# A causal attention block: the mask of the transposed scores comes with the shift that starts the score bank, instead of from a product on TensorE

## The reference, cut to what matters

```
x: (1, 2048, 256), H = 16 heads, D_NOPE + D_ROPE = 192, D_V = 128
h      = layernorm(x) * (1 + ca) + sa
q, k   = low-rank projections of h, with rotary parts     # 16 heads, 192 wide
scores = einsum('bhsd,bhtd->bhst', q, k) * scale
scores = where(tril(ones(seq, seq)), scores, finfo.min)    # causal: key t <= query s
attn   = softmax(scores, axis=-1)
out    = einsum('bhst,bhtd->bhsd', attn, v);  x = x + ga * (out @ w_o)
# then a second norm and a mixture of 8 experts, 2 per token
```

## Time and profile before

| | us |
|---|---|
| median of 3 runs (1333.61 to 1336.11) | 1335.11 |
| the profiled execution, its own time | 1335.97 |
| its span | 1334.2 |
| PE busy in the span | 1212.8 (91%) |
| DVE busy | 887.8 (67%) |
| ACT busy | 790.3 (59%) |
| POOL busy | 689.4 (52%) |

### The profile page before, as it was taken

One profiled execution on the slowest core, in us unless ns is written; L12 is line 12 of the kernel. 1 busy time (PEld: TensorE's weight loads), 2 busy tenths in 40 slices (PEclk: granted clock), 3 DMA queues, 4 the chain that ended last, 5 costly groups with the idle time before them and its releaser, 6 DMA issues. The chain is left out here.

```text
span 1334.2 us, 24515 instructions
## 1 busy us (share of the span) xinstructions
PE 1212.8 (91%) x9452; PEld 959.9 (72%) x9452; DVE 887.8 (67%) x1836; ACT 790.3 (59%) x1166; POOL 689.4 (52%) x569
## 2 busy tenths in 40 slices
PE   2766999999999999999999999999999958989897
PEld 2654577777777677777777777777777757878786
DVE  2533667777676777767667776766767476677776
ACT  1152577677777777777776777777777633322232
POOL 0121376677666657676665767666686741111100
PEclk9876799999999999999999999999999978999998
DMA  9201002001000200100020010002000040000000
GB/s 275 75 0 57 16 1 57 2 17 41 17 17 1 57 1 17 42 17 17 2 57 1 17 42 17 17 2 57 1 17 1 2 158 1 1 16 0 16 16 16
DMA packets 57671, 39.54 MB, mean 30 GB/s; under 512 B 7744, under 2 KB 57152, under 8 KB 57408
## 3 DMA queue, kind: packets, MB, share of 16 engines
q1 hardware_dynamic: 51216, 33.94, 8.7%
q10 hardware_dynamic: 6352, 4.19, 1.3%
HBM read 33.66 MB, written 4.46 MB: 29 GB/s over the span
## 5 line engine op out<-in xcount | busy, mean ns | idle before, releaser
L768 DVE TENSOR_REDUCE gates<-bank 128x1 f32<-128x512 f32 (+3 forms) x640 | 384.8, 609 | 225.7 <-PE bank L841 149.4
L660 POOL TENSOR_TENSOR pt_lo<-pt 128x1024 f16<-128x1024 f32 x192 | 372.7, 1946 | 241.8 <-ACT pt L717 240.5
L717 ACT ACTIVATE pt<-pair 128x1024 f32<-128x1024 f32 x192 | 196.1, 1021 | 130.1 <-PE pair L866 129.1
L708 ACT ACTIVATE pair<-shift 128x1024 f32<-128x1024 f32 x256 | 263.4, 1029 | 11.9
L884 PE MATMUL bank<-values,pt 128*128 128x129 f16 x2176 | 235.2, 222 | 9.4 <-DVE rowsum L800 9.3
L884 PEld LDWEIGHTS bank<-values,pt 128*128 128x128 bf16 x2176 | 191.5, 97 | 61.7 <-issue 31.8
L886 PE MATMUL bank<-values,pt_lo 128*128 128x65 f16 x2176 | 223.9, 193 | 0.0
L666 POOL TENSOR_TENSOR pt_lo<-pt 128x512 f16<-128x512 f32 (+3 forms) x256 | 178.8, 720 | 58.9 <-ACT pt L721 58.4
L886 PEld LDWEIGHTS bank<-values,pt_lo 128*128 128x128 f16 x2176 | 193.8, 98 | 0.0
L721 ACT ACTIVATE pt<-pair 128x512 f32<-128x512 f32 (+3 forms) x256 | 111.3, 436 | 77.4 <-PE pair L869 77.1
L841 PE MATMUL bank<-kt_a_hi,q_hi 128*128 128x512 f32 (+2 forms) x320 | 132.4, 419 | 4.4 <-ACT q_hi L690 2.4
(11 more groups left out here) (217 smaller groups left out, 2341.1 us busy)
## 6 DMA issues: line engine op xcount, KB each, us to landing
turn_by<-rope_cos_by_feature SPq DMA_DIRECT2D x64, 128.0 KB, 3.0
turn_by<-rope_sin_by_feature SPq DMA_DIRECT2D x64, 128.0 KB, 3.0
xs<-in_L_attn_x ACTq DMA_DIRECT2D x1, 2048.0 KB, 25.2
lat<-in_L_attn_w_o SPq DMA_DIRECT2D x1, 2048.0 KB, 26.6
xs_again<-in_L_attn_x SPq DMA_DIRECT2D x1, 2048.0 KB, 8.1
out<-xs_again SPq DMA_DIRECT2D x4, 512.0 KB, 2.8
lat<-in_L_wmod SPq DMA_DIRECT2D x1, 1536.0 KB, 16.1
lat<-in_L_attn_w_qb SPq DMA_DIRECT2D x1, 1152.0 KB, 8.0
```

Source lines behind the costliest of these rows:

```text
L660: pool.tensor_tensor(out=pt_lo[:, at].rearrange("p a n -> p (a n)"), in0=full, in1=cut(full), op=ALU.subtract).then_inc(low_ok, 1)
L708: act.activation(s_pair[u % 2][:, :, :], shift[:, item % SHIFTS:item % SHIFTS + 1, :].to_broadcast([P, 2, BW]), ACT.Copy).then_inc(seeded[ ...
L717: act.activation(pt[:, at], s_pair[u % 2][:, :, :], ACT.Exp).then_inc(exp_done, 1)
L768: dve.tensor_reduce(out=mx[:, item % MAXIMA, t, part:part + 1], in_=work_of(w)[:, 0:n * P], axis=AXX, op=ALU.max).then_inc(work_seen["v"], 1)
```

## The change

The 256 mask products (L869) go. In their place the shift that starts a score bank already holds the mask in the triangle. POOL makes a transposed triangle `mask_t` once at the start of `attend`. After ACT has copied the shift of an item, DVE reads the same work bank again and writes `diag_shift` = shift + log(1024) + mask for all four query tiles (`diagonal_rows`, one 128x512 instruction per item). A work bank with a shift in it is therefore free for PE only when ACT and DVE have both read it. The seed of a `d = 0` unit on ACT is now three instructions (the shift for columns 256 and up of both halves, the shift for tile 1 of half 0, and the two triangle tiles from `diag_shift`); that of a `d = 2` unit on DVE is two (the two triangle tiles, and the shift for tile 3 of half 0). The `shift` tile has 3 slots instead of 4.

```diff
-PT_RING, SHIFTS, Q_SLOTS, MAXIMA = 4, 4, 3, 4
+PT_RING, SHIFTS, Q_SLOTS, MAXIMA = 4, 3, 3, 4
@@ seen_by
-    return {"max": "v", "shift": "a", "q": "va"}[use[0]] if use[0] != "q" or use[2] < 2 else ""
+    return {"max": "v", "shift": "av", "q": "va"}[use[0]] if use[0] != "q" or use[2] < 2 else ""
@@ attend
+        def diagonal_of(u):
+            d = UNITS[u][2]
+            return s_pair[u % 2][:, :, :].rearrange("p a (b n) -> p (a b) n", n=P)[:, d:d + BT + 2:BT + 1, :]
@@ POOL
+                pool.memset(mask_t[:, :], 0.0).then_inc(consts_ok, 1)
+                pool.wait_ge(consts_ok, 2)
+                pool.affine_select(out=mask_t[:, :], in_=mask_t[:, :], compare_op=ALU.is_ge, fill=MASKED, base=0,
+                                   pattern=[[1, P]], channel_multiplier=-1).then_inc(consts_ok, 1)
@@ ACT seed
-                    act.activation(s_pair[u % 2][:, :, :], shift[:, item % SHIFTS:item % SHIFTS + 1, :].to_broadcast([P, 2, BW]),
-                                   ACT.Copy).then_inc(seeded["a"], 1)
+                    if UNITS[u][2] is None:
...
+                    else:
+                        act.activation(s_pair[u % 2][:, :, 2 * P:], shift[:, at:at + 1, 2 * P:].to_broadcast([P, 2, 2 * P]),
+                                       ACT.Copy).then_inc(seeded["a"], 1)
+                        act.activation(s_pair[u % 2][:, 0, P:2 * P], shift[:, at, P:2 * P], ACT.Copy).then_inc(seeded["a"], 1)
+                        act.activation(diagonal_of(u), diag_shift[:, item % 2, 0:2, :], ACT.Copy).then_inc(seeded["a"], 1)
@@ DVE
+                def diagonal_rows(item):
+                    n = WORK[("shift", item)]
+                    dve.wait_ge(work_seen["a"], SEEN["a"][n + 1])
+                    if item >= 2:
+                        dve.wait_ge(seeded["a"], SEEDS["a"][FIRST_UNIT[item - 1]])
+                    dve.scalar_tensor_tensor(out=diag_shift[:, item % 2], in0=work_of(n).rearrange("p (t n) -> p t n", n=P),
+                                             scalar=math.log(P_SCALE), in1=mask_t[:, :].unsqueeze(1).to_broadcast([P, BT, P]),
+                                             op0=ALU.add, op1=ALU.add).then_inc(work_seen["v"], 1)
@@ DVE seed
-                    dve.tensor_copy(s_pair[u % 2][:, :, 2 * P:],
-                                    shift[:, item % SHIFTS:item % SHIFTS + 1, 2 * P:].to_broadcast([P, 2, 2 * P])).then_inc(seeded["v"], 1)
+                    dve.tensor_copy(diagonal_of(u), diag_shift[:, item % 2, 2:BT, :]).then_inc(seeded["v"], 1)
+                    dve.tensor_copy(s_pair[u % 2][:, 0, 3 * P:], shift[:, at, 3 * P:]).then_inc(seeded["v"], 1)
@@ DVE rounds, behind the maxima and the spread, ahead of query work and seed
+                    if r in SHIFT_AT:
+                        diagonal_rows(SHIFT_AT[r])
@@ PE scores
-                        last = pe.matmul(to, keys[a], q[b], start=False, stop=(m == 2 and d is None), skip_group_check=True)
-                    if d is not None:
-                        on = (d + half) * P
-                        last = pe.matmul(s_pair[u % 2][:, half, on:on + P], mask16[:, :], ident16[:, :], start=False, stop=True,
-                                         skip_group_check=True)
+                        last = pe.matmul(to, keys[a], q[b], start=False, stop=(m == 2), skip_group_check=True)
```

More of the change, by code:

```diff
@@ L115 @@
 OPS = [0, *itertools.accumulate(1 if d is None else 2 for _, _, d in UNITS)]
-SEEDS = {e: [0, *itertools.accumulate(seed_on_vector(u) == (e == "v") for u in range(NU))] for e in "av"}
+SEEDS = {"a": [0, *itertools.accumulate({None: 1, 0: 3, 2: 0}[d] for _, _, d in UNITS)],
+         "v": [0, *itertools.accumulate(2 * (d == 2) for _, _, d in UNITS)]}
 ENDS = [0, *itertools.accumulate(d is not None for _, _, d in UNITS)]
@@ L585, in attend @@
         nmx = sb(own, "nmx", [P, 2, BT])
+        diag_shift = sb(own, "diag_shift", [P, 2, BT, P])
+        mask_t = sb(own, "mask_t", [P, P], BF16)
         spread = sb(own, "spread", [P, 2, BT, P], F32R)
@@ L695, in shift_rows @@
                     if item >= SHIFTS:
-                        act.wait_ge(seeded["v"], item - SHIFTS + 1)
+                        act.wait_ge(seeded["v"], 2 * (item - SHIFTS + 1))
                     act.activation(shift[:, item % SHIFTS, :], work_of(n)[:, :], ACT.Copy,
@@ L707, in seed @@
                         act.wait_ge(opened, 1)
-                    act.activation(s_pair[u % 2][:, :, :], shift[:, item % SHIFTS:item % SHIFTS + 1, :].to_broadcast([P, 2, BW]),
-                                   ACT.Copy).then_inc(seeded["a"], 1)
+                    at = item % SHIFTS
+                    if UNITS[u][2] is None:
+                        act.activation(s_pair[u % 2][:, :, :], shift[:, at:at + 1, :].to_broadcast([P, 2, BW]),
+                                       ACT.Copy).then_inc(seeded["a"], 1)
+                    else:
+                        act.activation(s_pair[u % 2][:, :, 2 * P:], shift[:, at:at + 1, 2 * P:].to_broadcast([P, 2, 2 * P]),
+                                       ACT.Copy).then_inc(seeded["a"], 1)
+                        act.activation(s_pair[u % 2][:, 0, P:2 * P], shift[:, at, P:2 * P], ACT.Copy).then_inc(seeded["a"], 1)
+                        act.activation(diagonal_of(u), diag_shift[:, item % 2, 0:2, :], ACT.Copy).then_inc(seeded["a"], 1)
                 def exponentials(u):
```

2 lines of the change are left out of this document (1 added, 1 removed).

## The result

Over 13 runs each the changed kernel has a median of 1337.84 us (1335.68 to 1339.36), the kernel before 1335.08 us (1333.01 to 1336.67). The ratio is 1.0019, 95% interval [1.0012, 1.0026]. The forecast was 1350, slower by 1.1%; the sign was right, the size was not, and 1337.8 lies inside the stated range and outside what the forecast called its own. A sign that hangs on 2.8 us between two terms of some 20 each was luck: the prediction's terms were not known that well.

A forecast was written before the change was run, and what follows sets the result against it. PE was taken as the bound, busy 898 of 914.5 us, with DVE level in rounds with a query product. 19 us gained on PE and 33 lost to DVE's queue made +14 on 1335.97: 1350 us, range 1334 to 1364.

The forecast's parts named there:

- What leaves PE: On PE, 256 mask matmuls at 0.12 us go; those not hidden in waits were to gain 19 us.
- What DVE gets: On DVE, one new 128x512 instruction per item, 64 in all, taken as 0.75 us each.
- rival C: The new DVE instruction takes 1.05 us in the mean: 1360 us, or 1369 with some at 2.38; chance 0.13.
- ACT's longer seeds: On ACT, `d = 0` seeds take 0.23 us more, 64 times, 15 us of busy time; costed at nothing.
- Rival D: ACT's longer seeds reach the path, 15 us more: 1365 us; chance 0.06.
- What DVE's place in the queue costs: DVE waits for ACT's shift copy, delaying the next maximum and PE: 4.7 us per head pair, 7 times, 33 us.
- the 32nd item: Fifth stall of a head pair: the seed is 0.85 late and a shift product waits about 0.5 us.
- the one too many: Four query-product stalls in each of 7 head pairs made 28 places; there are 27, the first shift being made ahead.
- the 0.13 between the maximum and the query product: On PE, the query product starts 0.13 us behind DVE's maximum; about 0.07 of that was taken as slack.
- The last head pair: It has no queries to prepare for a next pair, so the 4.7 us stall was counted 7 times only.
- the first class: 59 diagonal units in rounds with neither shift nor query product; both masks count, 0.24 us each, 14.2 us gained.
- Rival B: The delay reaches PE at about half size because waits overlap: 33 falls to 16, 1333 us; chance 0.13.

The follow-up runs named there:

- e1_no_mask: The kernel before without the 256 mask products of the scores and nothing in their place, so the causal mask is left out: 1312.4 us, ratio 0.9838.
- e7_split_seeds: The kernel before with only the seeds split as in the change (three pieces on ScalarE, two on VectorE), mask products kept: 1333.8 us, ratio 0.9991.
- e6_rows_twice: The changed kernel with the new VectorE instruction issued twice, the second waiting for the first: 1390.1 us, ratio 1.0410 to the kernel before.
- e8_late_seed_all: The changed kernel with VectorE's seed after the next first maximum behind four shifts per head pair, the last pair included: 1314.8 us, ratio 0.9847 to the kernel before.
- e2_rows_only: The changed kernel with mask products back on PE and seeds as before; the new VectorE instruction's output is unused: 1357.8 us, ratio 1.0180 to the kernel before.

## Why the prediction was right in its mechanism and wrong in its size

**What leaves PE: right.** 19 were predicted; the unstalled rounds of the changed kernel gave 10.1 + 6.5 = 16.6, and e1_no_mask 22.3 with nothing in the way, where 20 of the 27 rounds kept a gain of 0.12 as well. A mask at 0.12 is confirmed wherever it counts. The Trainium skill's 81 ns for each (TensorE: Matmul & The Clock Gate, Back-to-back issue gap) is too small for these places; as a mean over all 256, with those that fall into waits, the chip gives 22.3 / 256 = 0.087.

**What DVE gets: right.** 0.69 against 0.75, and rival C (1.05) is out: the longest of the 64 is within 0.01 of it. The Trainium skill's rule for a PSUM source (VectorE: DVE Perf Modes, The TRN2 errata) gave an estimate of 0.66 and is 0.03 under the row.

**ACT's longer seeds: right**, by e7_split_seeds. Rival D is out.

**The step that failed: "What DVE's place in the queue costs".** The wait was right, and so were the places but for the 32nd item and the one too many; the sum of a head pair was not. 4.7 us were forecast. In the changed kernel the four rounds are 0.72, 0.29, 1.00 and 0.72 longer where 1.1, 0.7, 1.35 and 1.05 stood, each 0.33 to 0.41 less, and the fifth place, the 32nd item, loses nothing. The 27 places together are 9.9 us less than forecast, the 28th, which does not exist, is 1.1, and the fifth is 3.5 more. Against them stand 2.6 us of gain reckoned and not had, and 1.1 at the first unit. -9.9 - 1.1 - 3.5 + 2.6 + 1.1 = -10.8, and the forecast's +13.7 becomes +2.9.

The 0.4 is in the one term that was added at each place: ScalarE's end to the start of the maximum, reckoned as 1.65 + 0.31 = 1.96 (1.65 where no output stands between). The rows above have 551.05 to 552.61, which is 1.56. Piece by piece: hand-over from ScalarE 0.04 for 0.1; from the start of the new instruction to that of the copy behind it 0.61 for 0.85; the two copies 0.52 for 0.70; the output 0.39 for 0.31. I had added durations and put a hand-over between them. VectorE's rows overlap instead: in these rows each starts some 0.08 to 0.10 before the end of the one in front. The earlier trace rows were durations, and the words ahead of the prediction, that on VectorE they follow each other nearly end to end, are off by that much. What a queue costs is the distance between starts, as I had said of PE and not done for DVE.

Two readings of the code and the rows were wrong as well. The copy behind the new instruction does not read what that one writes: in such a round the new instruction works for the next item, while the seed is for the `d = 2` unit of the present one, so the copy reads the other slot of `diag_shift`, and the second hand-over had no cause. And the 0.13 between the maximum and the query product was no slack: in the changed kernel, where PE stood idle for 1.04, the product starts as far behind (552.61 + 0.69 = 553.30, and 553.44). So with 0.40 less in the chain the maximum is 1.41 - 0.40 = 1.01 late, and PE loses 1.00.

An instruction that does wait for the one in front starts 0.03 behind its end. The pair of e6_rows_twice does (511.80, 511.83), and so do all 20 of the 64 negated maxima (L792 in the changed kernel) that wait for the reduction right in front of them. Of the 44 that wait for an earlier one, 37 start 0.07 to 0.08 before its end and 7 start 0.03 behind it, which this does not explain. The Trainium skill (VectorE: DVE Perf Modes, The DRAIN you can't avoid) says that the next operation does not start until the pipeline is empty, that one which isn't held back starts earlier, and that a semaphore costs nothing extra. The overlap agrees with the second; the third does not hold for these rows, where waiting for the instruction in front costs 0.11.

**The last head pair** was taken as free of stalls, since no query products follow there. Against e1_no_mask the changed kernel loses 0.45, 0.25, 0.77, 1.01, 0.34 and 0.53 there, in the rounds behind the shifts of its 1st, 2nd, 4th, 5th, 6th and 7th item: 3.3 us, 3.0 after what one round gives back. It is most of the 4.1 by which the first class fell short. The rows name three waits. The first is DVE's queue once more: the first product with the values (L910) waits for the output to leave its bank, here behind the 4th item's shift.

```profile
1012.50 0.69 DVE L806 SCALAR_TENSOR_TENSOR diag_shift<-bank,mask_t 128x512 f32<-128x512 f32 x1 [0.69 <-ACT shift L708]
...
1013.96 0.15 DVE L828 COPY rowsum<-bank 128x2 f32<-128x2 f32 x1
...
1014.17 0.23 PE L910 MATMUL bank<-values,pt 128*128 128x129 f16 x1 [0.36 <-DVE rowsum L828]
```

That product falls 0.45, 0.60 and 0.56 further behind e1_no_mask at the 1st, 4th and 5th item, and in e8_late_seed_all this wait is gone. The second is the work bank: the second chunk comes 0.17, 0.17 and 0.37 late at the 2nd, 4th and 5th, and at the 5th PE's row names the second reader. The third is a seed: at the 7th PE waits 1.51 for it instead of 0.97. The prediction counted none of them in this head pair.

**Rival B** named this outcome most closely: half the delay, with the turning point at 2.7 us for a head pair. Measured are 0.72 + 0.29 + 1.00 + 0.72 = 2.73, at that point. But its reason, that waits overlap with others that are there, is not what happened: e2_rows_only, with the masks in place, has 0.79 + 0.38 + 1.09 + 0.79 = 3.05 where 4.2 was forecast for these four, so the delays are small from the start.

## What to carry to other kernels

When two terms of opposite sign nearly cancel, an error of 0.4 us in one of them, times its count, is the whole answer: read such a chain from starts of neighbouring rows, on every engine, never from durations and an allowance. A new instruction that waits for another engine costs its queue the wait as well as the work, so look for what is in the queue behind it and could stand in front; here one moved line was worth 14 us and two moved lines 22. When a buffer gets a second reader, both the place in the queue and the hold on the buffer have to be reckoned, for curing one brings out the other.

## What the runs showed of the hardware

In the changed kernel a VectorE instruction that does not wait for the one in front mostly starts 0.07 to 0.09 us before that one's end, where its work is there: after the 0.69 us of L806 the copy starts 0.61 behind its start. One that waits for the one in front starts 0.03 after its end, so the same instruction twice, the second waiting for the first, is 0.72 apart (e6_rows_twice). From the end of ScalarE's copy to the VectorE instruction that stands waiting for it are 0.03, from the end of a maximum to the matmul that stands waiting for it 0.15. A 128-column bf16 matmul between fp32 ones costs TensorE 0.12 at full clock, of which only 0.04 stands at its own row; the rest makes the fp32 product behind it longer, 0.31 instead of 0.23.
